# Pre-norm decoder block on one core: paired transposes and whole head products in the cross-attention turns

## The reference

```
x = x + attention(layernorm(x), Wq, Wk, Wv, Wo)          # 16 heads of 128
# cross attention over the channel-major view: 8 heads of 64 rows
q = layernorm(x).reshape(4, 8, 64, 512); k = v = ctx.reshape(4, 8, 64, 512)
sm  = softmax(einsum('bhdq,bhdl->bhql', q, k) / 8)
x = x + gamma * einsum('bhql,bhdl->bhdq', sm, v).reshape(4, 512, 512)
# gated feed-forward, weights rounded to -1, 0, 1 times their mean magnitude, hidden 1365
h = layernorm(x)
x = x + (silu(h @ w1q.T) * (h @ w3q.T)) @ w2q.T
```

## Time and profile before

| | us |
|---|---|
| three runs | 1130.19, 1131.79, 1132.29 (median 1131.79) |
| the profiled execution: its own time | 1132.07 |
| the profiled execution: its span | 1130.2 |
| busy in the span: PE, DVE, ACT, POOL | 1111.2, 731.0, 542.2, 478.3 |
| chain that ended last: share of PE | 89% |

### The profile page before, as it was taken

One profiled execution on the slowest core, in us unless ns is written; L12 is line 12 of the kernel. 1 busy time (PEld: TensorE's weight loads), 2 busy tenths in 40 slices (PEclk: granted clock), 3 DMA queues, 4 the chain that ended last, 5 costly groups with the idle time before them and its releaser, 6 DMA issues.

```text
span 1130.2 us, 15803 instructions
## 1 busy us (share of the span) xinstructions
PE 1111.2 (98%) x5804; PEld 940.3 (83%) x5804; DVE 731.0 (65%) x1357; ACT 542.2 (48%) x1129; POOL 478.3 (42%) x420
## 2 busy tenths in 40 slices
PE   8999999999999999999999999989999999999998
PEld 6888888878888888888888888878787878888886
DVE  7555547777757588866424434679867976787532
ACT  3556673324142376677514323267627753775130
POOL 0222327341332275664434030266627762875131
PEclk9999999999999999999999999999999999999999
DMA  7465553545433634212631022362113211310000
GB/s 242 161 184 188 183 180 122 166 126 172 124 121 126 206 96 141 84 38 94 240 112 45 30 100 61 135 176 65 48 44 114 58 48 57 113 47 2 38 1 37
DMA packets 54663, 122.19 MB, mean 108 GB/s; under 512 B 10057, under 2 KB 10057, under 8 KB 52538
## 3 DMA queue, kind: packets, MB, share of 16 engines
q1 hardware_dynamic: 54586, 121.18, 33.2%
HBM read 103.32 MB, written 17.84 MB: 107 GB/s over the span
## 4 chain that ended last, share of the span: by engine, by line
PE 89%; DVE 4%; POOL 2%; DMA 1%; issue 1%; ACT 1%; SPq 0%; POOLq 0%; DVEq 0%; ACTq 0%
PE bank L161 19%; PE bank L162 19%; PE bank L163 19%; PE bank L562 5%; PE bank L563 5%; PE bank L520 4%; PE bank L577 4%; PE bank L578 4%; PE bank L530 2%; PE bank L544 2%; PE bank L545 2%; PE bank L531 2%; DMA x1d<-x_scratch 1%; POOL kl L909 1%; POOL qst L913 1%
## 5 line engine op out<-in xcount | busy, mean ns | idle before, releaser
L562 PE MATMUL bank<-x3h,w 128*128 128x512 f32 (+2 forms) x368 | 143.0, 392 | 0.4 <-DVE x3l L839 0.3
L563 PE MATMUL bank<-x3l,w 128*128 128x512 f32 (+2 forms) x368 | 140.1, 384 | 0.0
L1419 ACT ACTIVATE yh<-bank 128x512 fp32r<-128x512 f32 x64 | 38.1, 600 | 209.9 <-PE bank L163 209.9
L2025 POOL TENSOR_TENSOR wal<-raw_a,wah 128x512 fp32r<-128x512 f32 x44 | 60.5, 1401 | 137.5 <-ACT wah L1441 137.5
L754 DVE TENSOR_REDUCE xmx<-bank 128x1 f32<-128x512 f32 x128 | 87.6, 686 | 42.7 <-PE bank L531 41.4
L919 POOL TENSOR_SCALAR pe_x<-pe_x,xri,gam 128x512 f32<-128x512 f32 x96 | 75.6, 788 | 88.6 <-DVE xri L758 85.6
L2030 POOL TENSOR_TENSOR wbl<-raw_b,wbh 128x512 fp32r<-128x512 f32 x64 | 87.6, 1393 | 36.1 <-ACT wbh L1462 35.9
L161 PE MATMUL bank<-wah,gh 128*128 128x512 f32 x256 | 102.6, 401 | 0.0
L161 PE MATMUL bank<-yh,rh 128*128 128x512 f32 x256 | 100.2, 391 | 0.8 <-DVE xacc L1887 0.8
L1717 DVE TENSOR_TENSOR yl<-bank,yh 128x512 fp32r<-128x512 f32 x64 | 44.1, 691 | 86.8 <-ACT yh L1419 86.6
L162 PE MATMUL bank<-wal,gh 128*128 128x512 f32 x256 | 100.1, 391 | 0.0
(11 more groups left out here) (168 smaller groups left out, 2990.2 us busy)
## 6 DMA issues: line engine op xcount, KB each, us to landing
raw_a<-in_wk SPq DMA_DIRECT2D x8, 1024.0 KB, 5.6
raw_b<-in_wq SPq DMA_DIRECT2D x8, 1024.0 KB, 6.7
raw_a<-in_wo SPq DMA_DIRECT2D x8, 1024.0 KB, 5.2
raw_b<-in_wvt SPq DMA_DIRECT2D x8, 1024.0 KB, 5.2
ternary_scratch<-wraw SPq DMA_DIRECT2D x24, 341.2 KB, 3.0
x1d<-x_scratch SPq DMA_DIRECT2D x48, 128.0 KB, 2.9
kd<-in_ctx SPq DMA_DIRECT2D x48, 128.0 KB, 2.9
w<-ternary_scratch SPq DMA_DIRECT2D x2, 2730.0 KB, 10.9
```

The source lines that it names most:

```text
L562: pe.matmul(u_bank[w][0:m, cols], lhs, x3h[:, c, cols], start=c == 0, stop=False)
L563: mm = pe.matmul(u_bank[w][0:m, cols], lhs, x3l[:, c, cols], start=False, stop=c == CK - 1)
L2025: pool.tensor_tensor(wal[:, c, :], raw_a[:, c, :], wah[:, c, :].bitcast(F32), ALU.subtract).then_inc(s["wal_pool"], 1)
```

## The change

TensorE transposes tiles q and q+1 of head h-1 together in the even steps and none in the odd ones. A head's output becomes one product of eight matmuls 512 columns wide (`pe_ret_whole`) at q = 3 of the next head, and waits for all four tiles of its head. ScalarE converts tile q, does the exponential, then converts tile q+1; VectorE does both low parts in the even step, and adds a head's output at q = 1 behind the maximum instead of at q = 2 ahead of it. Heads 3 and 7 are prepared one step earlier; values are split in steps 1, 10, 18 and 26. In the first turn W2's load goes out ahead of the wait for `vd` and of `vd`'s load. The interleaved attention of sequence 0 keeps its half products.

```diff
         def values_step(h):
-            return 4 * h + (h % 4 == 0)
+            return 4 * h + 2 if h else 1
         def prep_step(h):
-            return 4 * h + (h % 4 == 2) if 0 < h < XH - 1 else None
+            return 4 * h if 0 < h < XH - 1 else None
...
+        def r_done(b, h):
+            return 2 * h + 2 if b == 0 else 2 * XH + (b - 1) * XH + h + 1
...
-            sp_head(sp, main, 1, 2)
+            sp_head(sp, main, 1, 2, values=False)
             sp_w2(sp)
+            sp_vd(sp, main, 1, 2)
...
+        def pe_ret_whole(pe, m, b, h):
+            pe.wait_ge(s["t_free"], t_p(b, h, 3) + 1)
+            if h % 2 == 0:
+                pe.wait_ge(s["vtl"], b * V_TILES + h // 2 + 1)
+            pe_wait(pe, "r_free", b * XH + h, 1)
+            for c in range(CK):
+                lhs = m.vts[:, h % 4, c, :]
+                pe.matmul(m.r[:], lhs, m.pxh[:, c, :], start=c == 0, stop=False)
+                mm = pe.matmul(m.r[:], lhs, m.pxl[:, c, :], start=False, stop=c == CK - 1)
+            mm.then_inc(s["r_ready"], 1)
...
                         pe_sx(pe, main, b, h, q)
-                        if h:
+                        if h and q % 2 == 0:
                             pe_pt(pe, main, b, h - 1, q)
-                        if q == 1 and h >= 2:
-                            pe_ret(pe, main, b, h - 2, 1)
-                        if q == 3 and h >= 1:
-                            pe_ret(pe, main, b, h - 1, 0)
+                            pe_pt(pe, main, b, h - 1, q + 1)
+                        if h and q == 3:
+                            pe_ret_whole(pe, main, b, h - 1)
...
                 pe_pt(pe, main, b, XH - 1, 0)
-                pe_ret(pe, main, b, XH - 2, 1)
                 pe_pt(pe, main, b, XH - 1, 1)
             if f is not None:
                 pe_down(pe, f, 0, range(0, HC // 2))
             if b is not None:
                 pe_pt(pe, main, b, XH - 1, 2)
+                pe_pt(pe, main, b, XH - 1, 3)
             if f is not None:
                 pe_down(pe, f, 0, range(HC // 2, HC))
             if b is not None:
-                pe_pt(pe, main, b, XH - 1, 3)
-                pe_ret(pe, main, b, XH - 1, 0)
+                pe_ret_whole(pe, main, b, XH - 1)
...
-                    if h:
+                    if h and q % 2 == 0:
                         act_px(act, main, b, h - 1, q)
                     act_exp(act, main, b, h, q)
+                    if h and q % 2 == 0:
+                        act_px(act, main, b, h - 1, q + 1)
...
-                    if q == 2 and h >= 2:
+                    dve_max(dve, main, b, h, q)
+                    if q == 1 and h >= 2:
                         dve_ret(dve, main, b, h - 2)
-                    dve_max(dve, main, b, h, q)
...
-                    if h:
+                    if h and q % 2 == 0:
                         dve_px(dve, main, b, h - 1, q)
+                        dve_px(dve, main, b, h - 1, q + 1)
```

More of the change, by code:

```diff
@@ L402, in rows, with sp_vd, sp_head @@
             return t[b]
-        def sp_head(sp, m, b, h):
+        def sp_vd(sp, m, b, h):
+            if h or b > 1:
+                sp.wait_ge(s["vtl"], b * V_TILES + h // 2)
+            sp.dma_start(m.vd[:], rows(ctx_cols, b)[h // 2]).then_inc(s["vd_in"], 16)
+        def sp_head(sp, m, b, h, values=True):
             slot, n = h % 2, b * XH + h
@@ L414, in sp_head @@
                 sp.dma_start(m.kd[part, slot, :], rows(ctx, b)[XD * h:XD * (h + 1), :]).then_inc(s[f"kd_in{slot}"], 16)
[L415 to L418, removed]
+            if h % 2 == 0 and b > 0 and values:
+                sp_vd(sp, m, b, h)
         def sp_values_early(sp, h):
@@ L614, in pe_turn @@
             if b is not None:
-                pe_pt(pe, main, b, XH - 1, 3)
-                pe_ret(pe, main, b, XH - 1, 0)
+                pe_ret_whole(pe, main, b, XH - 1)
             if f is not None:
[L618 to L622, removed]
+                pe_down(pe, f, 1)
                 pe_down(pe, f, 2)
@@ L664, in act_vt @@
             else:
-                act.wait_ge(s["r_ready"], 2 * (b * XH + h - 3) + 2)
+                act.wait_ge(s["r_ready"], r_done(b, h - 3) if h >= 4 else r_done(b - 1, XH + h - 3))
             act.activation(high, values, ACT.Copy).then_inc(s["vth"], 1)
@@ L762, in dve_ret @@
             rows_ = slice(XD * (h % 2), XD * (h % 2) + XD)
-            dve.wait_ge(s["r_ready"], 2 * n + 2)
+            dve.wait_ge(s["r_ready"], r_done(b, h))
             dst = m.x2[rows_, h // 2, :]
@@ L869, in dve_turn @@
                 dve_px(dve, main, b, XH - 1, 0)
+                dve_px(dve, main, b, XH - 1, 1)
                 dve_ret(dve, main, b, XH - 2)
-                dve_px(dve, main, b, XH - 1, 1)
                 dve_px(dve, main, b, XH - 1, 2)
+                dve_px(dve, main, b, XH - 1, 3)
                 dve_moments(dve, main, b, TJ - 2)
@@ L879, in dve_turn @@
             if b is not None:
-                dve_px(dve, main, b, XH - 1, 3)
                 dve_ret(dve, main, b, XH - 1)
@@ L945, in pool_turn @@
                         pool_prep(pool, main, b, h + 1)
-                    if values_step(h // 2 * 2) == n - 1:
-                        pool_vt(pool, main, b, h // 2 * 2)
+                    if n - 1 in map(values_step, range(0, XH, 2)):
+                        pool_vt(pool, main, b, (n - 1) // 8 * 2)
                 if f is not None:
@@ L1491, in act_v_early @@
             if g >= 2:
-                act.wait_ge(s["r_ready"], 2 * (2 * g - 3) + 2)
+                act.wait_ge(s["r_ready"], r_done(0, 2 * g - 3))
             act.activation(high, values, ACT.Copy).then_inc(s["vth"], 1)
```

## The result

The changed kernel takes 1174.11 us (median of four runs, 1170.73 to 1175.14) against 1131.97 for the kernel before on the same chip: ratio 1.037, 95% interval 1.036 to 1.039, 42 us slower. The forecast was 1177, range 1146 to 1196. The profiled execution took 1170.73 us with a span of 1168.9.

A forecast was written before the change was run, and what follows sets the result against it. TensorE, busy nearly all of the span and holding 89% of the chain that ended last, was taken as the bound. From 1132.07: - 12.5 - 1.2 + 51.6 + 7 = 1177 us, range 1146 to 1196.

The forecast's parts named there:

- Waits removed, 12.5 us: TensorE's waits in three turns for head preparations and one addition, with emptied array and slow clock: 12.5 us gained.
- Pairs at 0: TensorE's transposes: eight together take 0.89 us against twice 0.44 for four, so pairing saves 0.
- Whole product, 1.2 us saved: TensorE's product per head: eight 512-column matmuls instead of sixteen of 256 save 0.05 us, 1.2 over 24 heads.
- The new wait, 51.6 us: TensorE waits for tile 3 before the whole product at q = 3: 17.2 us a turn, 51.6 in three.
- The clock, +7: TensorE's granted clock falls behind some of the 21 new waits, at 1.6 us each: 7 us added.
- The rival "floor only": VectorE's backlog vanishes at the new waits: 1134 us, up to 1137 with preparation waits partly left; chance 8%.

The follow-up runs named there:

- experiment 1: The kernel before with only the preparations of heads 3 and 7, the values and W2's load moved: 1120.09 us, ratio 0.990.
- experiment 2: The changed kernel with the whole product undone (half products, additions at q = 2), transposes still in pairs: 1124.87 us, ratio 0.994.
- 7: The changed kernel with the additions of a head to x2 in the turns covering 8 of 512 columns: 1159.59 us, ratio 1.025.
- 6: The changed kernel with ScalarE converting both tiles of a pair ahead of the exponential: 1155.84 us, ratio 1.022.
- experiment 5: The changed kernel with VectorE's reciprocals moved up behind the maximum and nothing else: 1181.43 us, ratio 1.044.
- Experiments 3: The changed kernel with the whole product put off past the step's piece and the next step's scores: 1149.44 us, ratio 1.016.
- 4: The changed kernel with the product put off likewise, and VectorE's reciprocal moved up behind the maximum, ahead of the addition: 1134.99 us, ratio 1.004.

## Why the prediction was right, point by point

- **Waits removed, 12.5 us.** Measured by experiment 1: 11.5, with one wait left in turn 1 that loses 1.0. Turn by turn it is as counted: 2.8 in turn 2, and 5.9 in turn 1, where 6.9 less that 1.0 stood. The 0.3 added to each wait and the 1.6 for the clock were needed: the bare totals of the earlier trace rows are 9.1.
- **Pairs at 0.** On TensorE itself right: eight transposes span 0.79 us from their first start to the scores (870.60 to 871.39). But I did not ask when GpSimd has the second tile's share ready, and at five heads a turn it comes late and waits inside the pair (the eight of 882.17 last 1.32 instead of 1.03). That costs 4.1 us in the changed kernel, and experiment 2 puts the pairs at 5 us, a term that I had at zero.
- **Whole product, 1.2 us saved.** Not seen by itself. Behind a wait it takes 1.95 us, no less than the two halves' 1.90, because its second start is 0.33 behind the first instead of 0.23; only the last head's, without a wait, took 1.85. So 21 products a run cost 0.05 more each, 1 us, instead of saving it. The term is lost in the waits that it brought. The Trainium skill's smaller saving (TensorE: Matmul & The Clock Gate, Back-to-back issue gap; 0.5 by estimate) can't be told from the rows' 1.2 by the time of any run here.
- **The new wait, 51.6 us.** The mechanism is shown: experiment 2 takes it away, 7 and 6 change it by the backlog and by the order. The size was 42.8, so the forecast was 9 too high. Head by head 2.0, 2.9, 2.2, 1.9, 3.6, 2.9, 1.7 were forecast and 2.3, 2.3, 1.5, 1.3, 3.3, 1.8, 1.2 measured in turn 2. At head 1 I had counted both engines as free and was 0.3 too low: VectorE's late maximum of step 5 had pushed back ScalarE's exponential and queries. Elsewhere I was 0.3 to 1.1 too high: at head 2 TensorE arrived 0.3 later, held by the transposes inside the pair, and the tile was ready 0.4 sooner.
- **The clock, +7.** Two falls, 3 us, in the profiled execution. Its mean granted clock was 0.996; the three others had 0.991 to 0.993 and took 2.5 to 4.4 us more, so the median's share is nearer the 7: with two falls at 0.996 and ten at 0.984 (experiment 5) an estimate of four to five falls, 6 to 8 us. The 7 itself was a half of a half and not derived, so that it fits is luck. Turns 2 and 3 had waits of up to 3.3 us without a fall.
- **The sum.** 1132.07 - 12.5 + 42.8 + 3 + 4.1 (pairs) + 1 (products) = 1170.5 against 1170.73 of the profiled execution. At 1177 a size too high (the waits, by 9) stood against two too low (the pairs, by 4, and the products, by 2). The mechanism and the place were right; that the number came within 3 us of the median is in part luck.
- **The rival "floor only"** asked whether the preparation would be the next limit. Experiments 3 and 4 show that it would: 19.5 us of it hid behind the product's waits.

The best kernel is experiment 1, 1120.09 us: the preparations, values and loads of this change without its pairs and products.

## What to carry to other kernels

When a consumer is moved from data two steps old to data one step old, write out the path from producer to consumer operation by operation and hold it against the consumer's arrival in the step with the least work between; an engine that is idle 18% of the time (VectorE was busy for 66.6 of 81.7 us in the steps of turn 2 before) can still be three microseconds late at one place. Do the same for the producer of each tile when two are taken together: the second one's lateness was worth 4 us here. A wait hides every shorter one behind it, so removing it brings the next one out (39.4 us of idle time went, 19.5 came), and a fix for the hidden one shows its worth only then. Take a bundle apart: here one part was worth 11.5 us and the others cost 54.

## What the runs showed that I had not expected

The clock's falls depend on small shifts. With losses of 1.2 to 3.7 us at each wait, the changed kernel's profiled execution had two falls in the turns; the same kernel with its reciprocals moved had ten, with losses of 1.2 to 3.3. Each fall costs about 1.5. A wait is then worth more than its own length, by an amount that a single profile gives only roughly.
